# Two attention stages written out image by image, without the engines' loop over images

## What is computed

```python
# layer 0 (layer 1 alike: no bias of distance, its own inner layernorm, one expert for each token)
h = layernorm(x) * (1 + ca) + sa                    # sa, ca, ga ... from the image's condition c
q, k, v = split(h @ W_qkv.T + b_qkv)                # 16 heads of 8
scores = q @ k.T / sqrt(8) - slope[head] * abs(i - j)
x = x + ga * (softmax(scores) @ v @ W_out.T + b_out)
h = layernorm(x) * (1 + cb) + sb
g = softmax(h @ Wr); w, idx = top_k(g, 2)           # the two best of 8 experts
x = x + gb * sum(w[e] * relu(h @ W1[e]) @ W2[e] for e in idx)
```

## Time and profile before

| | |
|---|---|
| median of 3 runs | 2234.33 us (2229.03 to 2234.86) |
| profiled execution, its own time | 2232.88 us |
| its span, first to last instruction | 2231.1 us |
| busy: PE, DVE, ACT, POOL | 74%, 70%, 44%, 39% |
| mean granted TensorE clock | 0.914 |

### The profile page before, as it was taken

The page is one execution under the profiler, slowest core; times in us unless marked ns, Lnnn a source line. Parts: engine busy times, 40 slices in busy tenths (PEclk is TensorE's granted clock), DMA queues, the critical chain, the costliest instruction groups (busy, mean ns, idle before and its releaser), DMA issues. The chain is left out here.

```text
span 2231.1 us, 50544 instructions
## 1 busy us (share of the span) xinstructions
PE 1661.4 (74%) x14050; PEld 1157.3 (52%) x14050; DVE 1568.6 (70%) x4981; ACT 987.5 (44%) x1807; POOL 880.4 (39%) x932
## 2 busy tenths in 40 slices
PE   2488887888888845999953777777777777808885
PEld 1255555555555625989851444444444444406664
DVE  4478877878788735666635888888888889625554
ACT  0265655655566521222211555555555555602332
POOL 0223534434354342444433334444444444313433
PEclk7699999999999977999985999899999999959999
DMA  4333333334333313222235454444544544343332
GB/s 137 52 60 71 73 73 71 69 65 75 69 73 76 70 39 79 67 67 69 64 119 102 88 104 102 107 101 99 115 95 95 118 96 108 65 150 92 105 101 63
DMA packets 267387, 191.98 MB, mean 86 GB/s; under 512 B 26095, under 2 KB 257297, under 8 KB 266468
## 3 DMA queue, kind: packets, MB, share of 16 engines
q1 hardware_dynamic: 251880, 155.28, 33.3%
q0 software_dynamic: 15360, 35.03, 5.1%
HBM read 95.21 MB, written 53.18 MB: 67 GB/s over the span
## 5 line engine op out<-in xcount | busy, mean ns | idle before, releaser
L889 DVE TENSOR_REDUCE mx<-A 128x2 f32<-128x512 f32 x1024 | 685.2, 681 | 201.1 <-PE A L1149 179.1
L743 ACT ACTIVATE probs<-B 128x1024 f32<-128x1024 f32 x512 | 523.5, 1023 | 392.2 <-PE B L1169 195.7
L1149 PE MATMUL A<-stack 126*128 126x256 bf16 x2048 | 397.9, 284 | 168.4 <-DVE mx L889 134.2
L1169 PE MATMUL B<-stack 128*128 128x256 bf16 x2048 | 365.7, 281 | 61.1 <-DMA stack<-mrow 60.1
L1149 PEld LDWEIGHTS A<-stack 126*128 126x128 bf16 x2048 | 164.3, 100 | 335.3 <-DVE mx L889 240.3
L1187 PE MATMUL M<-probs,vals 128*32 128x256 f32 x4096 | 296.1, 407 | 27.2 <-DVE On L912 24.0
L1169 PEld LDWEIGHTS B<-stack 128*128 128x128 bf16 x2048 | 199.4, 102 | 122.2 <-DMA stack<-mrow 35.4
L1583 PE MATMUL B<-xtT,w1s 128*128 128x256 f32 x896 | 219.0, 395 | 39.4 <-DVE xtT L1464 32.6
L644 POOL TENSOR_TENSOR h<-xn,back_rows 128x256 f32<-128x256 f32 x64 | 46.3, 724 | 506.1 <-DVE xn L844 506.1
L658 POOL DMA_INDIRECT gathered<-h,slot_in x192 | 187.0, 974 | 101.3 <-DVE slot_in L1035 52.6
L1592 PE MATMUL A<-w2s,hid 128*128 128x128 f32 x1792 | 219.9, 276 | 5.5 <-issue 5.3
(11 more groups left out here) (183 smaller groups left out, 2503.2 us busy)
## 6 DMA issues: line engine op xcount, KB each, us to landing
stack<-parts SPq DMA_DIRECT2D x768, 64.0 KB
xt<-gathered SPq DMA_DIRECT2D x112, 132.0 KB
probs<-gathered SPq DMA_DIRECT2D x40, 256.0 KB, 2.8
w<-in_w SPq DMA_DIRECT2D x4, 2048.0 KB, 9.9
back_rows<-mod_rows SPq DMA_DIRECT2D x64, 128.0 KB, 3.7
x_mid<-X SPq DMA_DIRECT2D x64, 128.0 KB, 1.9
hid<-expert_out SPq DMA_DIRECT2D x64, 128.0 KB
X<-in_x SPq DMA_DIRECT2D x32, 128.0 KB
```

Of the source, the lines that this page charges most:

```text
L743: act.activation(probs[c % 4][:, :, :, :], Bp[c % 2][:, :, :, :], ACT.Exp, scale=EXP_SCALE[l][c // 4]).then_inc(b_exp.handle, 1)
L889: dve.tensor_reduce(mx[u][:, h, :], A[h % 2][:, :, :], AX.X, ALU.max).then_inc(a_max.handle, 1)
L1149: ins = pe.matmul(A[h % 2][:, t, :], stack[u][0:n, h, 0, t * P:(t + 1) * P], stack[u][0:n, h, 1, :], start=True, stop=True)
L1169: ins = pe.matmul(Bp[c % 2][:, j, t, :], stack[u][:, h, 1, t * P:(t + 1) * P], stack[u][:, h, 0, :], start=True, stop=(l == 1))
```

## The change

The loop goes. `run_ticks` calls `tick` for all 40 ticks in turn, each with i a number, so every image, semaphore count and address is a constant; an engine passes from one tick to the next without a jump. The arguments that carried the chains' counts through the loop go with it. The steps, their order within a tick, the buffers and the waits stay as they are. `Chain` keeps its methods for the expert stages' loops. (Lines behind the removed ones stand 18 lower in the changed kernel.)

```diff
-DVE_MARKS = (96, 134)
...
-LEAD, LAG, UNROLL, FIRST = 3, 5, 4, 6
-
-
-def run_ticks(eng, tick, ch=None, per=0):
-
-
-
-    def peeled(i):
-        return lambda off, n=2: (i + off, (i + off) // n, (i + off) % n) if 0 <= i + off < B else None
-
-    for i in range(-LEAD, FIRST):
-        tick(peeled(i))
-    times = (B - FIRST - LEAD) // UNROLL
-    if ch:
-        ch.before()
-    with eng.Fori(0, times) as k:
-        if ch:
-            ch.loop(k, per)
-        for i in range(FIRST, FIRST + UNROLL):
-            tick(lambda off, n=2: (k * UNROLL + (i + off), k * (UNROLL // n) + (i + off) // n, (i + off) % n))
-        if ch:
-            assert ch.n == per, ch.n
-    if ch:
-        ch.done(times)
-    for i in range(FIRST + UNROLL * times, B + LAG):
-        tick(peeled(i))
+LEAD, LAG = 3, 5
+
+
+def run_ticks(tick):
+
+
+
+    for i in range(-LEAD, B + LAG):
+        tick(lambda off, n=2: (i + off, (i + off) // n, (i + off) % n) if 0 <= i + off < B else None)
 
 
...
-            run_ticks(sp, tick)
+            run_ticks(tick)
...
-            run_ticks(pool, tick, ch, UNROLL * (7 if l else 5))
+            run_ticks(tick)
...
-            run_ticks(act, tick, ch, UNROLL * (5 if l else 3))
+            run_ticks(tick)
...
-            run_ticks(dve, tick, ch, DVE_MARKS[l])
+            run_ticks(tick)
...
-            run_ticks(pe, tick)
+            run_ticks(tick)
```

## The result

The changed kernel takes 2178.47 us in the median of 4 runs (2170.63 to 2182.37), the kernel before 2234.6 us in the median of 4 beside it: a ratio of 0.9746, with a 95% interval of 0.9711 to 0.9781. The same kernel in a later set of runs gave 2185.8 us (5 runs; ratio 0.977, 0.9753 to 0.9787). The profiled execution took 2179.04 us, with a span 54.0 us shorter than before.

What follows compares the result with a forecast made beforehand. It took the PE-DVE score exchange in the attention stages, stalled at DVE's jumps back, as the bound. Layer gains of 26.4 and 15.0 us, together 41.4, off 2232.88 us gave 2191.5, stated as 2192 us; range 2179 to 2212 us.

Steps and rivals of the forecast that it cites:

- The sum, layer 0: Layer 0's images 6 to 25: loop time less five times the four written-out images behind it, 455.90 - 5 x 85.90 = 26.4 us.
- The parts of layer 0: Layer 0's share of the effects priced singly: DVE idle at four jumps back, slower images behind them, register work at nothing.
- visible gap: DVE idle before the negated maxima after each jump back, four times a layer: 11.8 us per layer, 23.6 us in all.
- aftermath: The image behind each jump back runs slower, partly at TensorE's lower clock: 2.4 us (layer 0) and 2.1 us (layer 1) per jump.
- register work: Loop sums for waits and addresses: nothing on SP, ACT, POOL; PE's 19.2 us in layer 1 not added, another wait replacing it.
- The sum, layer 1: Layer 1's images 6 to 25: loop time less five times the four written-out images behind it, 474.00 - 5 x 91.80 = 15.0 us.
- layer 1 at the pace of its first images: Rival: layer 1 runs like written-out images 3 to 5, 22.53 us each, gaining 23.4 us there; 2183 us, chance 0.09.
- the wait for the maxima's rows: PE's wait at layer 1's B scores for this row transfer, forecast to rise from 22.4 to some 29 us over 20 images.
- Only DVE pays regularly: At the jumps back only DVE loses time each round; PE's branches have a median of 211 ns, one of 4985 ns.
- Only the bare gap comes back: Rival: only DVE's idle time at the jumps back returns in both layers, 23.6 us; 2209 us, chance 0.15.
- The slower rival, fetches in the open: Written-out images in both layers expose instruction fetches to DVE, 2.78 us each, 20 of them costing 55.6 us; 2247 us, chance 0.05.
- Layer 1's bound: Most that layer 1's images 6 to 25 could gain: 23 us, from written-out images 3 to 5 at 22.53 us each.

Runs made afterwards that it cites:

- dve_alone: Against the kernel before: only DVE's ticks written out, in both layers, the other four engines keeping the loop; 2197.49 us, ratio 0.9814.
- dve_pe: Against the kernel before: DVE and PE written out in both layers, ACT, POOL and SP keeping the loop; 2189.58 us.
- pe_alone: Against the kernel before: only PE's ticks written out, in both layers, the other engines keeping the loop; ratio 0.9993.
- dve_pe_hint: Against the kernel before: loop kept on all engines, but DVE and PE announce the jump back early in the body; ratio 0.9838.
- all_but_pe: Against the kernel before: SP, ACT, POOL and DVE written out in both layers, PE alone keeping the loop; 2196.38 us.

## Why the prediction was right or wrong

**The sum, layer 0: right, 26.4 forecast, 26.5 measured.** Its written-out stretch was the right yardstick, because at a clock of 1.00 the images before it, once written out, run just as it does: twenty in 429.4 us, four in 85.8, which is 21.47 and 21.45 each.

**The parts of layer 0: wrong, though they seemed to support the sum.** They were 11.8 us of visible gap and 4 x 2.4 = 9.6 us of aftermath, 21.4, and nothing for register work. By the steps, before less change: at step 8 it is 2.85 + 3.42 + 2.81 + 2.79 = 11.9 us. At step 1, the four behind a jump against the loop's own 12.08, it is 1.95 + 2.41 + 1.17 + 1.22 = 6.8 us; the prediction had taken one pair of images, and the edges differ. The rest is what every step pays without a jump, 0.04 to 0.6 us, some 1.7 us a round and 8.3 in all. The three make 27.0; cut at the negations, as the steps are, the twenty images differ by 456.41 - 429.36 = 27.05 (26.5 when cut at the maxima). That third term is DVE's own but for about 1 us of PE's, shown by dve_alone and dve_pe. The prediction costed register work on SP, ACT, POOL and PE, and never asked for DVE's, the engine that it had named as the one that pays. For SP, ACT and POOL "nothing" was nearly right: 2.1 us.

The agreement of 41.6 and 41.4 us was two misses that cancel. By layers the parts were 21.4 against 26.4, and 11.8 + 4 x 2.1 = 20.2 against 15.0. Set side by side, that would have told that something was missing in the one and that the other was measured on the wrong stretch. In layer 1 it was the parts that came near: the eight images beside a jump took 200.7 us before and 180.5 in the change, 20.2 us less.

**The sum, layer 1: wrong, and this is the step that failed.** 474.00 - 5 x 91.80 = 15.0 us took one stretch of four images for the pace. They were no typical ones: over the 13 profiles here whose code there is the same they took 88.5 to 92.4 us, 90.3 in the mean, and 5 x 90.3 = 451.5 is what the written-out layer 1 takes. The loop's 474.0 was at the low end of its three values too. Between the two profiled executions layer 1 gave 22.4 us; means on both sides give 26.9 for 15.0. 26.4 + 26.9 from the 2232.88 us of the profiled execution is 2179.6, against 2179.04 for that of the change, but so close an agreement is luck: there 22.4 us came from the loop's images and 5.2 from the unchanged images 26 to 30. The prediction's own rows warned of it: the four images stood at 0.96 of the clock, and layer 0's at 1.00.

**The rival "layer 1 at the pace of its first images"** (2183 us, chance 0.09) has the number that came, 451.6 us for 20 x 22.53 = 450.6, but not the reason: PE's register waits, one in each image, would show in the twelve images away from the jumps, and these gave 2.2 us of the 26.9. The reason given against it fell too: that the wait for the maxima's rows would take the place of PE's 19.2 us of "issue" and rise to some 29. It stayed at 21.8. The weight loads at that line of the kernel before had this row too:

```profile
PEld B L1169 <- ACT probs L743: 16.2, 26, 1.5
```

With the 19.2 that is 35.4 us of idle; in the change it is the 33.8 of the maxima's rows. So at the weight loads the same idle time goes by another name, and the matmuls' own wait did not grow.

**"Only DVE pays regularly"**: right for the kernel as it stood (PE written out alone: 0.9993). But it named PE's one branch of 4985 ns and gave it no term. Such a stall cost little beside DVE's gap (steps 8 and 1 at the second jump: 15.17 + 14.49 = 29.7 us with it, 14.52 + 13.94 = 28.5 in pe_alone), and some 5 us as soon as the gap was gone. The change takes both, so the sum did not suffer.

**"Only the bare gap comes back"** fell: dve_pe_hint, which takes the gap and keeps the loop, still differs from the change by 11.7 us in layer 0. The Trainium skill, Runtime: NRT & Kernel Launch, "Instruction fetch mechanics", has a jump out of the window wait for its target. By that alone the change would have given the 23.6 us of this rival. The runs agree with the rule, since a jump announced early loses the gap (14.6 to 11.94 us at step 8), and show what comes on top: the aftermath of 6.8 us and the small pieces of 8.3 us in layer 0.

**The slower rival, fetches in the open**, did not come: 35 more large packets, and no wait of DVE for an instruction in layer 0's twenty images; the one of 0.8 us in image 27 is all there is in images 6 to 29 of either layer.

**The range** ended at 2179, from 28 and 23.4 us as the layers' most. Layer 1's bound was too tight for the same reason as its term: the pace was taken from one stretch at a time. The later 2185.8 us of the same kernel lies inside the range, so the end of the range was missed by chance as much as by reason; layer 1's term was short in both sets.

## What to carry to other kernels

Before a loop is written out, compare iterations that already are, but in more than one execution and stretch wherever the pace of equal work varies; and set the parts against the sum stage by stage, since totals can agree by chance. Cut the loop into the iterations beside a jump and the others: here that shows at once where its excess lies. Ask each engine for the gap behind its jump and for the small pieces in every round: where one engine's gap covers the others', writing out those others gives nothing by itself, and what they hid comes out when the first is removed. If the code must stay a loop, announcing the jump back on the engines that pay gave over half of it here (0.9838 against 0.977).

## What had not been expected of the hardware

- One instruction of 39 ns that announces the jump takes 2.6 us and more out of DVE's step at the jump (14.54 to 11.93), and on PE, with one of its own, the one branch of 5 us is gone (at most 253 ns).
- That PE branch, 4.7 to 5.0 us, comes once in each of the six profiles in which PE loops in layer 0 unannounced, at the second jump in four of them, at the third (dve_alone) and the fourth (all_but_pe) in the others; why only once stays open.
- Beside its jumps the loop costs layer 0 some 1.7 us a round of four images, most of it on DVE, in pieces of a tenth of a microsecond that no row of waits shows; only equal steps of two kernels laid side by side do.
- Layer 1's images keep falling to a lower clock here and there (22.0 us at 1.00, 24.7 at 0.93) even when PE's wait for the maxima's rows is filled with work (0.95 over images 6 to 25, with it and without).
